# A two-layer convolution and attention kernel: fewer loaded slabs, smaller left-over products, a second place for the hidden layer

## The reference

```
hdn = relu(w1[m] (64 x 144) @ piece m + b1)      # 64 hidden rows per model
x   = x + w2[m] (16 x 64) @ hdn + b2             # 16 channels per model
```

```
theta, phi, g = projections of x (128 x 512 each, plus bias)
attn = softmax(theta^T phi)        # 1024 x 1024 per image
y    = attn @ g
out  = batchnorm(w @ y + b) + x
```

## Time and profile before

| | |
|---|---|
| median of three runs | 1627.13 us (1621.52 to 1631.98) |
| profiled execution, its time | 1610.33 us |
| profiled execution, its span | 1608.5 us |
| TensorE busy | 1514.1 us, 94% |
| VectorE busy | 872.4 us, 54% |
| ScalarE busy | 764.5 us, 48% |
| GpSimd busy | 263.5 us, 16% |
| DMA, share of 16 engines | 69.4% |
| HBM read / written | 252.56 MB / 109.05 MB |
| mean granted clock of TensorE | 0.976 |

### The profile page before, as it was taken

The page is one execution under the profiler, slowest core; times in us unless marked ns, Lnnn a source line. Parts: engine busy times, 40 slices in busy tenths (PEclk is TensorE's granted clock), DMA queues, the critical chain, the costliest instruction groups (busy, mean ns, idle before and its releaser), DMA issues.

```text
span 1608.5 us, 23836 instructions
## 1 busy us (share of the span) xinstructions
PE 1514.1 (94%) x8324; PEld 843.1 (52%) x8324; DVE 872.4 (54%) x1200; ACT 764.5 (48%) x1205; POOL 263.5 (16%) x134
## 2 busy tenths in 40 slices
PE   7899989998999999999999999999999999999975
PEld 1264545645555465554645555465554645555455
DVE  1275463745638365463745637366463745637465
ACT  2445454544545454454545545454454544545442
POOL 0030120302103021120302103021120302104021
PEclk9999999999999999999999999999999999999998
DMA  9875966759577585966859487584966759577234
GB/s 289 234 231 165 293 218 212 268 169 286 193 250 267 160 297 167 286 235 186 282 170 321 170 250 259 163 301 162 292 235 193 272 167 301 191 241 250 85 128 160
DMA packets 179006, 361.84 MB, mean 225 GB/s; under 512 B 12336, under 2 KB 120880, under 8 KB 178992
## 3 DMA queue, kind: packets, MB, share of 16 engines
q1 hardware_dynamic: 178992, 361.66, 69.4%
HBM read 252.56 MB, written 109.05 MB: 225 GB/s over the span
## 4 chain that ended last, share of the span: by engine, by line
PE 77%; DMA 11%; DVE 4%; issue 3%; SPq 3%; ACT 2%; DVEq 0%; ACTq 0%
PE ps L421 23%; PE ps L441 8%; PE ps L432 7%; PE ps L457 5%; DMA x_lo<-rows_out 5%; PE ps L459 5%; PE ps L458 5%; DMA rows_out<-probs 4%; PE ps L487 4%; PE ps L489 4%; PE ps L488 3%; PE ps L501 2%; PE ps L472 2%; PE ps L473 2%; PE ps L474 2%
## 5 line engine op out<-in xcount | busy, mean ns | idle before, releaser
L421 PE MATMUL ps<-windows,w_main 128*64 128x512 f32 x2048 | 486.0, 607 | 23.5 <-ACT hidden L625 12.8
L943 POOL TENSOR_TENSOR probs<-probs,row_inv 128x1024 f32<-128x1024 f32 x128 | 262.8, 2063 | 1317.5 <-DVE row_inv L781 1317.5
L625 ACT ACTIVATE hidden<-ps,columns 128x512 f32<-128x512 f32 x512 | 315.0, 688 | 302.6 <-PE ps L432 169.5
L421 PEld LDWEIGHTS ps<-windows,w_main 128*64 128x64 f32 x2048 | 130.3, 136 | 311.1 <-issue 203.8
L648 ACT ACTIVATE probs<-ps,neg_max 128x1024 f32<-128x1024 f32 x128 | 142.7, 1115 | 185.2 <-DVE neg_max L775 164.8
L756 DVE SCALAR_TENSOR_TENSOR x<-ps,columns,windows 128x512 f32<-128x512 f32 x128 | 96.0, 750 | 215.8 <-PE ps L441 168.2
L775 DVE TENSOR_REDUCE neg_max<-ps 128x1 f32<-128x1024 f32 x128 | 154.6, 1208 | 55.1 <-PE ps L474 52.9
L802 DVE TENSOR_TENSOR x_lo<-x_lo,x_hi 128x1024 fp32r<-128x1024 f32 x128 | 171.1, 1346 | 14.1 <-ACT x_hi L655 13.8
L487 PE MATMUL ps<-x_hi,arena 128*128 128x256 f32 x512 | 152.0, 297 | 25.8 <-DVE arena L808 16.2
L441 PE MATMUL ps<-hidden,w2s 128*32 128x512 f32 x1024 | 142.5, 630 | 28.5 <-ACT hidden L625 28.5
L793 DVE STREAM_TRANSPOSE probs<-probs 128x1024 f32<-128x1024 f32 x128 | 156.3, 1231 | 16.5 <-POOL probs L943 10.9
(11 more groups left out here) (55 smaller groups left out, 1514.8 us busy)
## 6 DMA issues: line engine op xcount, KB each, us to landing
windows<-in_x SPq DMA_DIRECT2D x208, 562.0 KB, 12.7
rows_out<-probs SPq DMA_DIRECT2D x128, 512.0 KB, 3.9
x_lo<-rows_out SPq DMA_DIRECT2D x128, 512.0 KB, 4.2
out<-x SPq DMA_DIRECT2D x64, 512.0 KB, 3.5
windows<-in_x SPq DMA_DIRECT2D x32, 421.5 KB, 9.5
windows<-in_x SPq DMA_DIRECT2D x32, 409.9 KB, 11.0
windows<-in_x SPq DMA_DIRECT2D x32, 281.0 KB, 6.1
rows_out<-hidden SPq DMA_DIRECT2D x16, 512.0 KB, 4.5
```

The source lines that it names most:

```text
L421: mm(ps[rows, hidden_bank(s, q), :], w_main[:, p, which, :], shifted(windows[:, w, :], unit // UNITS, half), start=True, stop=False, skip_ ...
L625: activation(hidden[:, q, :], ps[:, hidden_bank(s, q), :], ACT.Relu, bias=b1s[:, column:column + 1]).then_inc(hidden_ready, 1)
L943: nc.gpsimd.tensor_tensor(rows, rows, row_inv[:, e].to_broadcast([P, PIXELS]), ALU.mult).then_inc(normalized, 1)
```

## The change

The left-over unit is chosen differently. For even pairs the first model's main product has units 0 to 3 and the second's 4 to 7 of the pair's nine; units 4 (for the first) and 8 (for the second) are left over. For odd pairs the mains have units 1 to 4 and 5 to 8, and units 0 and 4 are left over. Main products now start at even units only. So there are 7 slabs inside a shift (starting at units 0, 2, ..., 12) and 4 crossing ones: 11 instead of 19. A main's weight rows that belong to the other model are zero. In place of one product of 32 rows and 128 columns, each pair has two left-over products of 32 rows and 64 columns, one for each model, which read the same row quarter of the array. Their number in a slot goes from 4 to 8.

`hidden` gets two places, used by slots in turn, so relu of slot s waits for `dx` of slot s-2. `g_t` is a tensor of its own, and the wait for `g_sent` goes. `ROWS_HELD` goes from 3 to 4. Of the 11 slabs, group 0, 1 and 2 free one crossing slab each; group 3 frees the other 8, which are loaded at the start of the batch, 4 after the last group's sums and 4 after the last `sum_x1`. For the first image, rounding and splitting of the output weights (`ww_hi`, `ww_lo`) moves from behind the loop over the slots to inside it, ahead of the last slot.

The diff, cut to what matters (the changes of names from shared to left are left out where nothing else changes):

```diff
-ROWS_HELD = 3
+ROWS_HELD = 4
...
 def first_unit(p, which):
-    return PAIR_UNITS * p + (0 if which == FIRST else 5)
-def shared_unit(p):
-    return PAIR_UNITS * p + 4
+    return PAIR_UNITS * p + p % 2 + (0 if which == FIRST else 4)
+def left_unit(p, which):
+    return PAIR_UNITS * p + (0 if p % 2 else 4) + (0 if which == FIRST else 4)
...
-WINDOWS = INSIDE_ONE + 1 + len(CROSSING)
+INSIDE = INSIDE_ONE // 2 + 1
+WINDOWS = INSIDE + len(CROSSING)
 def window_of(unit):
     r = unit % UNITS
-    return r if r <= INSIDE_ONE else INSIDE_ONE + 1 + CROSSING.index(unit)
+    return r // 2 if r <= INSIDE_ONE else INSIDE + CROSSING.index(unit)
...
+SUMMED = [2 * _g for _g in range(GROUPS)]
...
-    _ws = [_w for _w in READ_ORDER if LAST_GROUP[_w] == _g]
-    _ws = [_w for _w in _ws if _w not in (4, 8, 12)] + [_w for _w in _ws if _w in (4, 8, 12)]
+    _ws = sorted((_w for _w in READ_ORDER if LAST_GROUP[_w] == _g), key=lambda w: w in SUMMED and (w + SUMMED[-1]) % (2 * GROUPS) + 1)
     FREED[_g] = (_ws[:(len(_ws) + 1) // 2], _ws[(len(_ws) + 1) // 2:])
...
-        hidden = sb("hidden", [P, GROUP_PAIRS, HALF])
+        hidden = sb("hidden", [P, 2, GROUP_PAIRS, HALF])
+        g_t = sb("g_t", [P, PIXELS])
-        w_shared = sb("w_shared", [P, GROUPS, 2 * HIDDEN])
+        w_left = sb("w_left", [P, GROUPS, 2, HIDDEN])
...
             def load_freed(n, grp, part):
-                sp.wait_ge(hidden_summed, ((n - 1) * SLOTS + GROUPS + grp + 1) * GROUP_PAIRS)
-                summed = [w for w in FREED[grp][part] if w in (4, 8, 12)]
-                if summed:
-                    sp.wait_ge(x1_ready, (n - 1) * SLOTS + GROUPS + max(summed) // 4 + 1)
+                if not FREED[grp][part]:
+                    return
+                if any(w in SUMMED for w in FREED[grp][part]):
+                    assert grp == GROUPS - 1
+                    sp.wait_ge(x1_ready, n * SLOTS)
+                else:
+                    sp.wait_ge(hidden_summed, ((n - 1) * SLOTS + GROUPS + grp + 1) * GROUP_PAIRS)
                 for w in FREED[grp][part]:
                     load_window(n, w)
...
                 for q in range(GROUP_PAIRS):
-                    unit = shared_unit(GROUP_PAIRS * grp + q)
                     rows = slice(UNIT * q, UNIT * (q + 1))
-                    mm(ps[:, hidden_bank(s, q), :], w_shared[rows, grp, :],
-                       shifted(windows[rows, plain_of(unit), :], unit // UNITS, half), start=False, stop=True,
-                       skip_group_check=True).then_inc(hidden_summed, 1)
+                    for which in (FIRST, SECOND):
+                        unit = left[q][which]
+                        last = mm(ps[HIDDEN * which:HIDDEN * (which + 1), hidden_bank(s, q), :],
+                                  w_left[rows, grp, which, :],
+                                  shifted(windows[rows, plain_of(unit), :], unit // UNITS, half), start=False,
+                                  stop=True, skip_group_check=True)
+                    last.then_inc(hidden_summed, 1)
...
             def relu(n, s, q):
                 act.wait_ge(hidden_summed, (n * SLOTS + s) * GROUP_PAIRS + q + 1)
-                if q == 0 and s > 0:
-                    act.wait_ge(dx_summed, n * SLOTS + s)
-                elif q == 2 and s == 0 and not (isinstance(n, int) and n == 0):
-                    act.wait_ge(g_sent, n * 16)
+                if q == 0 and (s > 1 or not (isinstance(n, int) and n == 0)):
+                    act.wait_ge(dx_summed, n * SLOTS + s - 1)
                 column = place_of(n, s) % GROUPS * GROUP_PAIRS + q
-                activation(hidden[:, q, :], ps[:, hidden_bank(s, q), :], ACT.Relu,
+                activation(hidden[:, s % 2, q, :], ps[:, hidden_bank(s, q), :], ACT.Relu,
...
-            act.wait_ge(ww_transposed, 1)
-            nc.scalar.copy(ww_hi[:, :], ps[:, BANK_Y, :]).then_inc(ww_rounded, 1)
+                elif s == SLOTS - 2:
+                    act.wait_ge(ww_transposed, 1)
+                    nc.scalar.copy(ww_hi[:, :], ps[:, BANK_Y, :]).then_inc(ww_rounded, 1)
...
             for s in range(SLOTS - 1):
+                if s == SLOTS - 2:
+                    dve.wait_ge(ww_rounded, 1)
+                    tt(ww_lo[:, :], ps[:, BANK_Y, :], ww_hi[:, :].bitcast(F32), ALU.subtract).then_inc(ww_split, 1)
                 sum_x1(0, s)
                 split_x1(0, s)
...
-            dve.wait_ge(ww_rounded, 1)
-            tt(ww_lo[:, :], ps[:, BANK_Y, :], ww_hi[:, :].bitcast(F32), ALU.subtract).then_inc(ww_split, 1)
```

More of the change, by code:

```diff
@@ L84 @@
     for _q in range(GROUP_PAIRS):
-        _w = plain_of(shared_unit(GROUP_PAIRS * _g + _q))
-        FIRST_READ.setdefault(_w, (_g, "shared", _q))
-        LAST_GROUP[_w] = _g
+        for _which in (FIRST, SECOND):
+            _w = plain_of(left_unit(GROUP_PAIRS * _g + _q, _which))
+            FIRST_READ.setdefault(_w, (_g, "left", _q))
+            LAST_GROUP[_w] = _g
+SUMMED = [2 * _g for _g in range(GROUPS)]
 for _g in range(GROUPS):
-    LAST_GROUP[4 * _g] = max(LAST_GROUP[4 * _g], _g)
+    LAST_GROUP[SUMMED[_g]] = max(LAST_GROUP[SUMMED[_g]], _g)
 READ_ORDER = list(FIRST_READ)
@@ L310, in send_g @@
                 sp.wait_ge(g_transposed, n + 1)
-                sp.dma_start(rows_out[QBLOCKS], g_t).then_inc(g_sent, 16)
+                sp.dma_start(rows_out[QBLOCKS], g_t[:, :]).then_inc(g_sent, 16)
             def fetch_g(n):
@@ L356, in _ @@
             for w in READ_ORDER:
-                if FIRST_READ[w] == (0, "shared", 0):
-                    sp.dma_start(w_shared[:, :, :], w_shareds).then_inc(w_shared_loaded, 16)
+                if FIRST_READ[w] == (0, "left", 0):
+                    sp.dma_start(w_left[:, :, :, :], w_lefts).then_inc(w_left_loaded, 16)
                     sp.dma_start(columns[:, :], per_channel).then_inc(columns_loaded, 16)
@@ L441, in dx @@
                     last = mm(ps[32 * q:32 * q + 32, BANK_DX, :], w2s[:, place_of(n, s) % GROUPS * GROUP_PAIRS + q, :],
-                              hidden[:, q, :], start=True, stop=True)
+                              hidden[:, s % 2, q, :], start=True, stop=True)
                 last.then_inc(dx_summed, 1)
@@ L757, in sum_x1 @@
                     in0=ps[:, BANK_DX, :].rearrange("p (h w) -> p h w", w=SIDE), scalar=b2s[:, grp:grp + 1],
-                    in1=shifted(windows[:, 4 * grp, :], 0, half), op0=ALU.add, op1=ALU.add).then_inc(x1_ready, 1)
+                    in1=shifted(windows[:, SUMMED[grp], :], 0, half), op0=ALU.add, op1=ALU.add).then_inc(x1_ready, 1)
             def split_x1(n, s):
@@ L796, in transpose_g @@
                 dve.wait_ge(proj_biased, n * 6 + 6)
-                nc.vector.transpose(g_t, g_t).then_inc(g_transposed, 1)
+                nc.vector.transpose(g_t[:, :], g_t[:, :]).then_inc(g_transposed, 1)
             def split_row(n, i):
@@ L972 @@
     w_mains = np.zeros((P, PAIRS, 2, HIDDEN), w1.dtype)
-    w_shareds = np.zeros((P, GROUPS, 2 * HIDDEN), w1.dtype)
-    for p in range(PAIRS):
+    w_lefts = np.zeros((P, GROUPS, 2, HIDDEN), w1.dtype)
+    for m in range(MODELS):
+        p, which = divmod(m, 2)
         grp, q = divmod(p, GROUP_PAIRS)
-        w_mains[:, p, FIRST] = w1[2 * p, :P]
-        w_mains[:, p, SECOND] = w1[2 * p + 1, WINDOW - P:]
-        w_shareds[UNIT * q:UNIT * q + UNIT // 2, grp, :HIDDEN] = w1[2 * p, P:]
-        w_shareds[UNIT * q + UNIT // 2:UNIT * (q + 1), grp, HIDDEN:] = w1[2 * p + 1, :WINDOW - P]
+        for unit, units, place in ((first_unit(p, which), P // UNIT, w_mains[:, p, which]),
+                                   (left_unit(p, which), 1, w_lefts[UNIT * q:UNIT * (q + 1), grp, which])):
+            start = UNIT * unit - WINDOW * m
+            a, b = max(0, start), min(WINDOW, start + UNIT * units)
+            place[a - start:b - start] = w1[m, a:b]
     w2 = np.asarray(L0_conv_w2).transpose(0, 2, 1).reshape(MODELS // 2, 2, HIDDEN, MODEL_CH)
```

47 lines of the change are left out of this document (24 added, 23 removed).

## The result

| | before | after |
|---|---|---|
| median | 1624.33 us (4 runs, 1617.78 to 1631.98) | 1571.32 us (4 runs, 1570.79 to 1572.14) |
| span of the profiled execution | 1608.5 us | 1569.0 us |
| DMA queue | 361.66 MB, 69.4% | 288.24 MB, 56.7% |

The changed kernel is faster: ratio 0.967, 95% interval 0.963 to 0.972. The forecast was 1588 us, from 1552 to 1613.

What follows compares the result with a forecast made beforehand. TensorE, busy 94% of the span, was taken as the bound. Waits 10, clock 15, left-over products 2 and first image 10 sum to 37 us; off the median that gives 1590, with a little surplus 1588 us, range 1552 to 1613.

Steps and rivals of the forecast that it cites:

- Slab traffic ahead of row 0: DMA queue: 11 slabs instead of 19 leave it empty for rows 0 and 1; waits fall 10 us, bounds 0 and 49.6.
- What is late next: TensorE, queue empty: row 1 leaves 1.6 us before dx, then g delays attend(0); 2.6 us of waits an image in all.
- Clock: From 100 to 1475 us the lower clock level costs 27 us; quiet images win back 15, bounds 0 and 27.
- Left-over products: TensorE's left-over groups: 8 products on row quarters and column halves run at once; -2 us, between -6 and 0.
- rival (c): Left-over products sharing a row quarter run one after the other: at least 115 us more, 1707 us; chance 0.13.
- Two places, own g, fourth row: Two places for hidden and own g_t give 0 us; the fourth row only repairs the disturbed image, already counted with the slabs.
- The first image: Shorter waits for slabs and weights, no 4.57 us wait before the first projection, some clock: 10 us, bounds 3 and 12.
- From the profiled execution to the median: The 37 us taken off the median gives 1590; a little of its 16.8 us surplus over the profiled execution makes 1588.

Runs made afterwards that it cites:

- e2: Kernel before, with 8 of the 19 slabs loaded at only 16 bytes per row in each DMA after the first image: 1586.78 us, ratio 0.9784.
- e5: Changed kernel with 8 DRAM copies of 0.575 MB issued for each of images 2 to 15, putting slab traffic back: 1593.50 us, ratio 0.984.
- e10: Changed kernel with no slab loaded in full after the first image, only 16 bytes per row in each DMA: 1571.30 us, ratio 0.970.
- e9: Changed kernel with the 8 DRAM copies of e5 and three held rows instead of four: 1591.14 us, ratio 0.983.
- e1: Kernel before, with only each shared product of 32 rows and 128 columns made as two of 64 columns: 1621.78 us, ratio 0.9989.
- e3: Changed kernel with one place for hidden instead of two, g keeping its own: 1572.02 us, ratio 0.968.
- e4: Changed kernel with three held rows instead of four: 1571.23 us, ratio 0.968.
- e6: Changed kernel with the output weights rounded and split behind the first image's slot loop again: 1577.31 us, ratio 0.974.
- e8: Changed kernel with row 7's scores before attend(0), exp 5 before rounding g, slot 0's dx behind row 6's scores: 1563.89 us, ratio 0.9636.
- e12: e8 with VectorE's transpose of row 4 moved behind y's split, row 3's split, the first output sum and max 7: 1634.49 us, ratio 1.0074.

## Why the prediction was right, point by point

- *Slab traffic ahead of row 0.* Right, and shown from both sides: taken out of the old kernel it gives 36 us (e2), put into the new one (64 of 73 MB) it takes 22 (e5), taken out wholly it gives nothing more (e10). Waits 49.6 to 40.9 us; 10 us were forecast for the gain, 8.7 came. One link was wrong: exp 3's wait for row 0's sending is real, but it does not end the chain (e9, and the rows of the kernel before beside it).
- *What is late next.* Right: waits of about 1.6 us for relu and 1 us for g were worked out from the last image, where no slabs are loaded, and a better one; after the change they average 19.3 / 15 = 1.3 and 20.8 / 15 = 1.4. The split was off, the sum of 2.6 us an image is nearly exact (2.7), and so is the 2.7 us from sending row 0 to its fetch.
- *Clock.* 15 us taken of 27. The clock went to 1.00 in the middle, and by periods it gave about 12. The 27 were too much to begin with: the clock records of the trace before have 48 us at the lower level between 100 and 1475 us, which is 24 us of loss at most, and in about 8 of the 48 TensorE waited anyway. The 15 was a choice between bounds, and its nearness is partly luck: the waits of 2.7 us an image that remain can still bring the clock down, as the last section shows for e10.
- *Left-over products.* Right: -2 us forecast, 0.027 us a group (3.5 us) seen, 3.4 us of group time in e1. The Trainium skill ("TensorE: Matmul & The Clock Gate", Part 3) gives about 4 ns for each further tile; by that a group would have been 31 ns shorter, an estimate from this figure and the earlier trace rows. The traces have 27. The same part of the Trainium skill says that a weight load overlaps a running product only when the row group differs. The runs do not agree for tiles on the same rows and different columns: rival (c), with its 115 us, did not come, and e1 has a ratio of 0.9989.
- *Two places, own g, fourth row: 0.* Right for the places and the row, by e3 and e4. The own place of g was not tried in the changed kernel, but e2, which has none of the three, leaves nothing for it.
- *The first image.* The mechanisms were right, the size too small: 10 us, of which 1.7 for clock; 13.4 came. The mains that start at 21.20 take 3.65 us, where those of before, at 22.98, took 6.20, at the lower clock. This term of 2.5 us was missing. It is in part luck: the same mains were slow (5.2 to 6.2 us) in the three traces with 19 slabs, but also in two of the eleven with 11 slabs (e6 and e8, 5.35 us), behind much the same waits as in the others. e6 bears out the 4.6 us of wait and some clock (6 us).
- *From the profiled execution to the median.* This is the step that was mis-sized, and it is why the forecast lies 17 us above what was measured. Span against span the sum of 37 us met 39.5. But I took the same 37 off the median and added 2 for its surplus of 16.8 us over the profiled execution. The surplus was disturbed images, as far as the traces tell. The profiled execution of e1, whose kernel times like the one before, took 1630.88 us, some 20 more than that of before, and has waits of 64.5 us where that had 49.6 and a lower mean clock (0.967 for 0.976). After the change the surplus is gone (the timed runs lie within 3.2 us of the profiled span), and the medians differ by 53 us. The supposition was written down and then given only an eighth of its worth (2 of 16.8).

## What to carry to other kernels

When TensorE is 94% busy and its waits differ from one loop pass to the next at the same place, look for a transfer that lands on top of another at that place: a pass that has no such transfer (here the last image) tells what will be left once it is gone. A wide spread of the runs can be part of the price of such a collision: it was 14 us with it, and 1.4 and 6.5 us in two measurements without. Here the profiled execution lay below the median, and what it showed of the price was too little. A step moved down a strictly ordered queue must be followed through every queue that it passes, as e12 shows: a wait of TensorE made 0.4 us an image shorter cost 71 us by way of a DMA and ScalarE.

## What the runs showed of the hardware

- Eight float32 products on tiles of 32 rows by 64 columns ran at once: 16 instructions in 1.05 us, against 8 on tiles of 32 by 128 in 1.07 us.
- It was the bytes and not the number of issues on SP: 16 bytes per row instead of whole slabs, with the same number of DMAs, gave 36 us in the kernel before (e2) and nothing once the queue was quiet (e10).
- The granted clock of the stretch from 100 to 1475 us was 1.00 in the changed kernel, whose waits there reach at most 1.8 us, and 0.98 in e12, where one wait of 2.8 to 2.9 us came in each image and mains behind it took 5.35 us instead of 3.65. But no length of wait that is safe can be read from this. Behind a wait of 1.82 us in the changed kernel the clock stayed up, and behind one of 1.80 us in e10 it fell (each wait with the stretch behind it, the changed kernel first):

```profile
480.70 0.39 PE L499 MATMUL ps<-x_hi,arena 128*128 128x256 f32 x1 [1.82 <-DVE arena L819]
481.00:491.00 10.00, 9.96 (x68) 7.96 (x67) 9.81 (x12) 4.62 (x7) 4.69 (x2) 1.00 0.38 127
```
```profile
672.96 0.39 PE L503 MATMUL ps<-x_hi,arena 128*128 128x256 f32 x1 [1.80 <-DVE arena L823]
673.00:683.00 10.00, 10.00 (x56) 8.21 (x57) 8.77 (x11) 3.47 (x5) 4.69 (x2) 0.83 0.32 109
```

What decides between the two is not shown here; part of what one execution pays for the clock differs from run to run.
